# Sixteen of the products by C of the first row on GpSimd in place of eleven, with weight copies and checks at other steps

## The reference

```python
xx, res = jnp.split(x @ in_w.T, 2, axis=-1)
xx = silu(conv4(xx) + conv_b)                     # 512 channels
delta, B, C = jnp.split(xproj(xx), [16, 32])
delta = softplus(delta @ dt_w.T + dt_b)
carry = exp(delta * A) * carry + delta * B * xx   # 16 states per channel, 512 steps
y     = sum_n(carry[n] * C[n]) + xx * D
x     = layernorm(x + (y * silu(res)) @ out_w.T)
h     = silu(x @ w1 * s1) * (x @ w2 * s2)
h     = gelu(h @ h1 * hs1); h = gelu(h @ h2 * hs2)
x     = layernorm(x + h @ w3 * s3)
```

## Time and profile before

| what | us |
|---|---|
| median of 3 runs (lowest, highest) | 2676.06 (2673.97, 2678.06) |
| the profiled execution, its own time | 2672.01 |
| its span | 2670.2 |
| PE, DVE busy | 2424.1, 2414.6 |
| ACT, POOL busy | 2101.0, 1605.4 |
| first scan of row 0 begins | 56.47 |
| first convolution tap of row 1 begins (behind pair 15) | 113.38 |
| closing of row 0's sum (line 981) begins | 192.65 |

### The profile page before, as it was taken

How to read it: one execution, slowest core, us unless ns; L and a number is a source line. 1 busy time by engine, 2 the same in 40 slices (tenths; PEclk the granted TensorE clock), 3 DMA queues, 4 the chain that set the end, 5 groups by cost and what they waited for, 6 DMA issues and landing times.

```text
span 2670.2 us, 36236 instructions
## 1 busy us (share of the span) xinstructions
PE 2424.1 (91%) x12098; PEld 1841.9 (69%) x12098; DVE 2414.6 (90%) x2388; ACT 2101.0 (79%) x3225; POOL 1605.4 (60%) x1561
## 2 busy tenths in 40 slices
PE   5677999989899998999999898998989999898988
PEld 2445776867767686776767677686767768676767
DVE  6899999999999999999999999999999999999730
ACT  5886987969798896978879697897969789696711
POOL 1336567666756766576566656666665676667554
PEclk7879999999999999999999999999999999999999
DMA  6858999989899898989989898998989899898933
GB/s 250 223 139 206 224 215 224 225 215 237 206 226 220 218 231 208 237 205 223 224 218 233 206 236 200 227 224 214 244 204 227 204 230 226 212 237 199 263 113 116
DMA packets 224491, 573.26 MB, mean 215 GB/s; under 512 B 25664, under 2 KB 26048, under 8 KB 223824
## 3 DMA queue, kind: packets, MB, share of 16 engines
q0 software_dynamic: 71424, 260.08, 51.9%
q1 hardware_dynamic: 152880, 310.84, 35.3%
HBM read 301.86 MB, written 20.45 MB: 121 GB/s over the span
## 4 chain that ended last, share of the span: by engine, by line
PE 39%; DVE 28%; DMA 10%; issue 9%; ACT 7%; POOL 7%; DVEq 0%; POOLq 0%; SPq 0%; ACTq 0%
PE ffn_ps L554 23%; DMA y<-hC 9%; DVE scan_ps L807 7%; PE scan_ps L435 6%; DVE hC L807 5%; PE misc_ps L440 4%; DVE hC L818 3%; DVE y L833 3%; PE misc_ps L499 2%; POOL ha_lo L1057 2%; PE misc_ps L484 2%; DVE gate L923 2%; ACT dA L657 2%; DVE stats L884 1%; POOL y L1016 1%
## 5 line engine op out<-in xcount | busy, mean ns | idle before, releaser
L807 DVE TENSOR_TENSOR_SCAN scan_ps<-dA,scan_ps 128x1024 f32<-128x1024 f32 x411 | 939.8, 2287 | 53.2 <-PE scan_ps L435 52.2
L1016 POOL DMA_DIRECT2D y<-hC x496 | 442.7, 892 | 716.7 <-DVE hC L818 505.8
L666 ACT ACTIVATE dB<-duT,bT 128x512 f32<-128x512 f32 x1024 | 710.9, 712 | 46.8 <-PE scan_ps L435 46.7
L657 ACT ACTIVATE dA<-delta,ch 128x512 f32<-128x512 f32 (+1 forms) x1024 | 681.4, 711 | 0.9
L554 PE MATMUL ffn_ps<-hb_hi,ring 128*128 128x512 f32 x1536 | 653.3, 425 | 28.4 <-DVE gate L923 17.3
L435 PE MATMUL scan_ps<-ident,dB 128*128 128x128 f32 x4096 | 559.8, 283 | 77.3 <-DVE hC L818 64.4
L435 PEld LDWEIGHTS scan_ps<-ident,dB 128*128 128x128 f32 x4096 | 487.3, 145 | 203.2 <-issue 73.3
L554 PE MATMUL ffn_ps<-hb_lo,ring 128*128 128x512 f32 x1536 | 609.9, 397 | 0.0
L818 DVE TENSOR_TENSOR hC<-scan_ps,c_rows_sb 128x1024 f32<-128x1024 f32 x411 | 501.0, 1219 | 45.0 <-DMA y<-hC 9.0
L554 PE MATMUL ffn_ps<-ha_hi,ring 128*128 128x512 f32 x1024 | 430.5, 420 | 0.0
L554 PE MATMUL ffn_ps<-ha_lo,ring 128*128 128x512 f32 x1024 | 401.4, 392 | 0.0
(11 more groups left out here) (103 smaller groups left out, 3178.4 us busy)
## 6 DMA issues: line engine op xcount, KB each, us to landing
y<-hC POOLq DMA_DIRECT2D x496, 512.0 KB, 6.3
ring<-rounded_weights SPq DMA_DIRECT2D x704, 256.0 KB, 4.9
c_rows_sb<-c_rows SPq DMA_DIRECT2D x256, 256.0 KB, 5.0
x<-ffn_w SPq DMA_DIRECT2D x22, 512.0 KB, 6.4
rounded_weights<-ffn_w SPq DMA_DIRECT2D x22, 512.0 KB, 6.7
xt<-x_chan SPq DMA_DIRECT2D x16, 512.0 KB, 4.0
xt<-x_tok SPq DMA_DIRECT2D x16, 512.0 KB, 5.3
out_st<-x_chan SPq DMA_DIRECT2D x16, 512.0 KB, 5.0
```

The lines of the kernel that those rows point to most:

```text
L657: nc.scalar.activation(dA[:, s % DA_RING, s % 2:], delta2[:, par, c, s % 2:], ACT.Exp, scale=a_neg[:, c, n:n + 1]).then_inc(dA_ready, 1)
L666: nc.scalar.activation(dB[:, n % 2, t, :], duT[:, t, :], ACT.Copy, scale=bT2[:, par, t, n:n + 1]).then_inc(dB_ready, 1)
L807: nc.vector.tensor_tensor_scan(states, dA[:, a:a + 2, :].rearrange("p a l -> p (a l)"), b, 0.0, ALU.mult, ALU.add).then_inc(scan_done, 1)
L1016: pool.dma_start(y2[:, par, c:c + 2, :], hC[:, slot], accum_op=ALU.add).then_inc(y_added[p % 2], 16)
```

## The change

Three tables of row 0 are replaced. GpSimd gets pairs 2, 5, 6, 8, 10, 13, 15, 30 and 31 and gives 4, 9, 14 and 18 to VectorE, so it has 16 rather than 11. `SUM_AT`, which is worked out from that table, moves with it. Of the checks the first comes four steps earlier, ahead of the second convolution; nine of VectorE's twelve still stand in iteration -1. Of the copies seven stand in iteration -1 in place of ten, and fifteen in iteration 0. The order of instructions from iteration 1 on is the same.

```diff
-PREP_AT = (-30, -27, -25, -24, -20, -12, -7, -5, -3, 2, 5, 12, 16, 17, 18, 20, 23, 26, 30, 33, 38, 39)
-COPY_AT = tuple(range(-26, -16)) + tuple(range(2, 62, 5))
+PREP_AT = (-34, -30, -25, -20, -19, -9, -7, -5, -2, 0, 2, 5, 9, 14, 19, 20, 21, 28, 29, 33, 44, 45)
+COPY_AT = (-20, -18, -16, -15, -13, -12, -7, 3, 10, 13, 25, 36, 37, 38, 39, 42, 44, 46, 51, 53, 56, 59)
...
-FIRST_POOL_PAIRS = (0, 3, 4, 9, 14, 16, 17, 18, 25, 27, 28)
+FIRST_POOL_PAIRS = (0, 2, 3, 5, 6, 8, 10, 13, 15, 16, 17, 25, 27, 28, 30, 31)
```

## The result

The changed kernel takes 2680.60 us (median of 12 runs, 2675.34 to 2683.69), the kernel before, run beside it, 2675.59 us (12 runs, 2671.50 to 2678.06). The ratio is 1.0017, interval 1.0009 to 1.0025: slower by 4.5 us by the ratio, with an interval of 2.4 to 6.7, and 5.0 us by the medians. I had forecast 2675.0 with a range of 2669.0 to 2680.5.

The account below looks back on a forecast made before the run. VectorE's multiplies, the serial odd transfers of row 0 and other DMA traffic were taken as the bound. +1.1 - 4.3 + 1.1 + 0 + 1.0 = -1.1 us gave a median of 2675.0, range 2669.0 to 2680.5.

Parts of the forecast that it names:

- Row 0's odd transfers as a second limit beside VectorE: Row 0: sixteen adding transfers of odd pairs run serially and take almost as long as VectorE's work.
- Rival B: Row 0's end and middle: copies crowd the transfer of pair 27 and delay pair 30; +6.8 us, 2682.9; chance 0.12.
- burst of copies: Middle of row 0, four copies issued at once at steps 36 to 39: booked as nothing, up to +2 us.
- Rival C: Pairs 0 to 15: other transfers fill the copies' space, so no shortening; +4.3 us, 2680.4; chance 0.12.
- the chain: Row 0's serial odd transfers: pair 3's issue to pair 11's landing, 40.4 us before, was to shorten by 5.4.
- part 4: End of row 0, pairs 30 and 31 on GpSimd: close 1.0 us later; bounds -2.7 to +3.3.
- the collision: Before row 1's first scan: VectorE's tensor_scalar waits out GpSimd's multiply of pair 30, ending 1.1 us later; not summed.
- Part 2: Pairs 0 to 15, GpSimd multiplying nine instead of five: gain of 4.3 us; bounds +1.1 to -7.1.
- Part 1: Startup, a weight check ahead of the second convolution, behind the first three taps: +1.1 us; bounds 0 to +1.2.
- Part 3: Middle of row 0: pair 18 back on VectorE, +1.1 us; the copies issued together there, nothing, up to +2.
- the start: Before row 0's first scan: the check between the taps makes that scan 1.1 us later.
- pair 18: Middle of row 0: its multiply returns to VectorE between taps, costing +1.1 us.

Follow-up runs that it names:

- after: The changed kernel with all three tables of row 0 replaced, against the kernel before: 2680.60 us, ratio 1.0017.

## Why the prediction was wrong

**What was right.** Row 0's odd transfers as a second limit beside VectorE, the scan of a GpSimd pair waiting for its slot, and GpSimd's in-order list as the way by which a late transfer delays pair 30. That pairs 30 and 31 lose rather than gain was forecast. Rival B names the place and the copies that make the transfer of pair 27 late, and I gave it 0.12; but its condition, a landing above 11 us, wasn't met (10.2), and its burst of copies cost nothing. Rival C's number, 2680.4, is next to the measured one by luck: it has the chain as long as before, which was shorter, and part 4 at +1.0.

**Part 4 failed, in its size.** I took +1.0 with an upper bound of +3.3. The profile has +4.8 (23.8 against 19.0), and the medians with and without the two pairs differ by 5.7. The wait was nearly as assumed: the transfer of pair 27 took 10.2 for 9.7, and the scan of pair 31 began 15.4 us behind that of pair 27, where I had 14.8. The term that failed is the collision behind it. I weighed it at 1.1 us of VectorE's time and left it out of the sum, and even that counted one GpSimd instruction. (By its own times it would have moved the close by 0.7, and the sum to -0.4 rather than the -0.2 that I gave.) It took 4.05 - 0.45 = 3.6, because VectorE's operation waited out both multiplies; with the operation moved, the median was 3.0 lower, which these runs don't tell apart from none. The Trainium skill, SBUF — State Buffer, "SBUF: two separate sides", has the rule that the loser waits for the whole instruction of the other; the trace agrees and goes further, since here it waited for two of them in a row, and in the run where the second could not yet start it took 0.49. A second term was wrong too, but hidden in after: TensorE's sum of pair 30 was priced at 1.88 from a row at full clock; after 6.2 us of waiting the clock was 0.50 and it took 3.78. It becomes 3.06 us of waiting on VectorE once the operation is moved. I had assumed that a stall changes only when something starts, not how long it takes.

**Part 2 failed, and hid behind the rest.** I took -4.3 for pairs 0 to 15; the profile has -0.6, and the pair table without 30 and 31 gained nothing in two table settings (2675.90 and 2674.93 against 2675.1 and 2675.3). The step that failed is the shortening of the chain by 5.4 us: from the issue for pair 3 to the landing of pair 11 it took 37.3 us in after, 3.1 less than the 40.4 of before, and 34.9 with the loads spread. I counted the copies and loads beside the chain as an average, but the changed `PREP_AT` puts three loads behind one wait of SyncE's list, so they start together beside the transfer of pair 9: 9.7 us, and a wait of 3.87 at the scan of pair 13. I looked for the wait only at pair 15. The price of 2.15 us per 512 KB was no constant either: beside the transfer of pair 27 the first copy added about 3.4 us and the second about 1. With the loads spread the stretch took 52.5 us, where my own sum had 52.6 (109.04 - 56.47), and the median was 3.0 lower, on the edge of what the runs tell. So the size I named was there to be had in that stretch, but not with this table.

**Part 1.** The check delayed the taps behind it by 1.1 us, as said; the end doesn't show it (2674.98 and 2674.93). **Part 3**, nothing from the burst of copies, holds: the transfer of pair 17 took 12.3 us (16.2 was my number), and undoing that changed nothing that the runs can tell.

The terms together: with part 2 at its measured zero and part 4 at +5.7, the sum is within a microsecond of the 5.0 that was measured, if the start and pair 18 are taken as unseen. That last is an inference; no run tests pair 18 alone, and the 5.7 is itself known only to some 3 us.

## What to carry to other kernels

When work is moved to GpSimd, ask which short operations of VectorE will stand beside it, and with how many instructions in a row; such a loss is booked as busy time and no list of waits shows it. When transfers form a serial chain, look at where each other transfer will really start, behind its own queue's waits, and not at the step in the table. And where a delay leaves TensorE waiting, look at the granted clock of what comes right after: here, behind waits of 5 to 6 us, the same products took twice as long.

## What the runs showed of the hardware

- A tensor_scalar of 0.45 to 0.48 us on VectorE took 2.85 us beside one GpSimd multiply and 4.05 and 4.06 beside two in a row, but 0.49 where GpSimd's second had to wait for a scan.
- TensorE's sum of four products: 1.88 us at a granted clock of 1.00, 1.98 after 1.59 us of waiting (clock 1.00), 3.78 at a granted clock of 0.50 after waits of 4.9 to 6.2 us. Four products of row 1 took 1.88 us at 1.00 and 3.23 to 3.44 at 0.55 to 0.58, in three runs where the sum had come late.
- The same 512 KB adding transfer landed after 4.5 us with nothing beside it (pair 25). For pair 27 it took 5.6 us with two C loads of 256 KB, 9.0 with these and one copy of 512 KB, 10.2 with these and two copies. For pair 9 it took 9.7 with three loads of 512 KB, two C loads and a copy, and for pair 17 12.3 with a C load and four copies.
- The same program's stretch from taps to pair 27 took 63.2 us in the profile of after and 58.8 in the run that differs from it only behind that stretch. Comparing one profile with one other would have blamed that stretch for 4 us.
